# Six weights handed over transposed, bias rows on four column strips, and first loads split over two queues

## The chip, the cores and the metric

The kernel runs on one core of a Trainium2 chip. It is one program for the core's five engines: TensorE (PE in the profile), VectorE (DVE), ScalarE (ACT), GpSimd (POOL) and SyncE (SP, which here only issues DMAs). The metric is the device time of one execution in microseconds (us), as the median of several runs.

## What is computed

The input is `x`, 128 graphs of 64 nodes with 512 features (8192 tokens of 512, f32), an adjacency `adj` of 128x64x64 and a node mask. Four layers follow one another. Each adds to `x` what it makes of `h = relu(layernorm(x))`:

```
layer 0: q, k = split(h @ Wqk); v = h @ Wv
         w = mask * sum(q * (adj @ (k * mask))) / sqrt(512); x += softmax_nodes(w) * v
layer 1: q, k, v = h @ W.T + b   (three weights)
         w = adj * exp(q @ k.T);  x += (w / rowsum(w)) @ v
layer 2: q, k, v = h @ W.T + b;  8 heads; softmax(q k.T / 8 * 2 adj) @ v;  x += ctx @ Wo.T + bo
layer 3: e = leaky_relu(sj + si + ab); T = rownorm(adj * exp(e))
         x += relu(h Wk0 + T h Wk1 + T T h Wk2 + biases)
```

Layers 1 and 2 use their weights transposed (`W.T`). Layer 0 uses `Wqk` only through the product of its q half and its k half.

## The kernel before, in words

The 8192 tokens are cut into 16 groups of 512 (`NG = 16`). Layers 0 and 1 run in one loop over the groups, layer 1 one group behind layer 0; layer 2 and layer 3 have a loop each. Every engine has its own hand-written program (`pe_program`, `dve_program`, `act_program`, `pool_program`, `sp_program`); the order of the work is the order of the code, and semaphores join the engines. Matmul results go to eight PSUM banks that are handed out in rotation (`Banks.take`); a bank is written again only when the engine that read its last contents has said so.

A large f32 product is made in three passes: each operand is split into a part `hi` (rounded to float32r by ScalarE) and a part `lo` (the rest, by VectorE or GpSimd), and hi*hi, hi*lo and lo*hi are added up (L319 where a weight is the left operand, L329 where features are). So each weight needs, once, a `hi` and a `lo`. For a weight that is used as it lies in HBM (`v0`, the layer-3 weights) this is `split_in_place`: `hi` from `raw`, and then `lo` over `raw`, which has the same memory. For `v1`, `q2`, `k2`, `v2` and `o2`, TensorE first transposes the weight block by block into four banks (`split_T`, 16 transposes of 128x128, L296), and the split reads the banks (`split_W`).

Features: `stats_A` (DVE) and `scale` (POOL) give mean and scale, `norm` (ACT, L1002) makes `hn`, `transposes` (DVE, L668) turns it in blocks of 32x32 to `hs`, `gather` (SP, L1430) moves 16 blocks of 64 KB to `hGA` (layers 0, 2, 3) or `hGB` (layer 1), and from there `hi` (ACT, L988) and `lo` (POOL L1248, or DVE L631 in layer 2) are made. TensorE then starts the group.

The start, ahead of the first group: TensorE transposes the q half and the k half of `Wqk` (32 transposes, L296), ScalarE copies them to `qT` and `kTw`, and TensorE forms `m0` = q half times k half (`product`, L309, 16 f32 matmuls that are not split). Then come a sum of bias products (L405), two rows of bias times weight (L411: eight matmuls whose left operand is one column wide), the first half of the layer-1 product `a1` (L309), and group 0 (`l01_g0`). The other half of `a1`, the transposes of `v1` and the two small products `crow` (L472) and `ucol` (L476) stand behind group 0's `v0`. The bias columns and the mask columns are also made by TensorE transposes (L397, L398, and L437 for layer 2).

At the end of the first loop, round `g == NG`, stand the last layer-1 group and the preparations of layer 2: the transposes of `q2`, the product `l01_pv(14)` (attention times values; L380, L384), `g1` of group 15 (L319), the transposes of `k2`, `v1` of group 15 (L329) and its scores (L345). In the layer-2 loop follow the transposes of `v2`, `l01_pv(15)`, and at the end of group 0 those of `o2`.

```
for half in range(2):
    pe.wait_ge((d_qk0, d_qk1)[half], 16)
    for cc in range(4):
        transposed_blocks(("qkT", half, cc), wqk[:, :, half * 512:(half + 1) * 512], cc, ...)
```

## Time and profile before

| | |
|---|---|
| median of 3 runs | 2275.75 us (2275.45 to 2278.11) |
| profiled execution, its own time | 2281.91 us |
| its span, first to last instruction | 2280.1 us |
| TensorE busy | 2246.0 us (99%) |
| VectorE, ScalarE, GpSimd busy | 1314.0, 784.9, 717.8 us |
| mean granted TensorE clock | 0.995 |
| DMA over the span | mean 99 GB/s |

A busy share is time with at least one instruction of the engine running. Matmuls overlap and their ends are modelled, so the distance from one start to the next tells more than the length of one. In the chain of waits each row is a start, a length and who held up the end; rows are merged over neighbours. The granted clock is 1.00 at 2.4 GHz and 0.50 at 1.2 GHz; at the very start of the program it reads 1.00 whatever happens.

### The profile page before, as it was taken

What the parts mean: (1) busy time and instruction counts of PE and PEld (TensorE: products, weight loads), DVE (VectorE), ACT (ScalarE), POOL (GpSimd) and SP (SyncE); (2) the same over time, 40 slices, a digit from 0 to 9 for tenths busy, and PEclk for the clock granted to TensorE, in tenths of its full rate; (3) what the DMA queues carried; (4) which work ended last, traced back from release to release, by engine and by line L of the source; (5) the groups of instructions that cost most, each with busy time, mean ns of one, the idle gap of its engine ahead of it and who ended that gap; (6) DMA issues with size and microseconds to landing.
All of it is one profiled execution on the core that took longest, in us unless ns stands there. A gap on an engine that the chain in (4) does not pass through costs nothing.

```text
span 2280.1 us, 39533 instructions
## 1 busy us (share of the span) xinstructions
PE 2246.0 (99%) x15903; PEld 1779.9 (78%) x15903; DVE 1314.0 (58%) x2645; ACT 784.9 (34%) x1401; POOL 717.8 (31%) x926
## 2 busy tenths in 40 slices
PE   8999999999999999999999999999899999999998
PEld 5778888888888877888888888888677777777776
DVE  3565565565655665554656455665665757575752
ACT  3332332333322333233333333232343434343432
POOL 2343343334333423223332223332351313131320
PEclk9999999999999999999999999999899999999999
DMA  6223333333333343332333332333444343535341
GB/s 199 75 75 96 96 107 102 84 92 94 84 95 96 102 135 111 99 101 80 85 101 92 101 97 80 91 105 93 123 123 111 84 114 82 129 68 127 71 106 37
DMA packets 185048, 224.75 MB, mean 99 GB/s; under 512 B 68688, under 2 KB 85152, under 8 KB 184864
## 3 DMA queue, kind: packets, MB, share of 16 engines
q1 hardware_dynamic: 179104, 214.35, 35.1%
q10 hardware_dynamic: 5760, 7.87, 1.4%
q8 instruction: 125, 2.05, 0.4%
q14 instruction: 59, 0.48, 0.1%
HBM read 88.91 MB, written 50.37 MB: 61 GB/s over the span
## 4 chain that ended last, share of the span: by engine, by line
PE 90%; SPq 3%; DVE 3%; DMA 2%; ACT 1%; issue 1%; POOL 1%; DVEq 0%; ACTq 0%
PE bank L329 49%; PE bank L319 28%; PE bank L345 3%; PE bank L603 3%; SPq L1430 2%; PE bank L533 1%; PE bank L503 1%; PE bank L309 1%; PE bank L380 1%; DMA si<-stB 1%; PE bank L296 0%; DVE hs L668 0%; DMA arows<-stB 0%; DMA small<-in_L_gnn_ab 0%; ACT g1T L1037 0%
## 5 line engine op out<-in xcount | busy, mean ns | idle before, releaser
L329 PE MATMUL bank<-w_hi,h3T_hi 128*128 128x512 f32 x768 | 306.4, 399 | 1.8 <-ACT Z L988 1.8
L329 PE MATMUL bank<-w_lo,h3T_hi 128*128 128x512 f32 x768 | 300.3, 391 | 0.0
L329 PE MATMUL bank<-w_hi,h3T_lo 128*128 128x512 f32 x768 | 300.0, 391 | 0.0
L1235 POOL TENSOR_SCALAR stA<-stA 128x4 f32<-128x4 f32 x48 | 11.5, 239 | 682.8 <-DVE stA L645 682.7
L1002 ACT ACTIVATE hn<-x,stA 128x512 f32<-128x512 f32 x192 | 140.7, 804 | 233.9 <-POOL stA L1240 228.0
L643 DVE BATCH_NORM_STATS2 stA<-x 128x6 f32<-128x512 f32 x192 | 128.3, 668 | 149.2 <-DMA x<-mid 148.8
L329 PEld LDWEIGHTS bank<-w_hi,h3T_hi 128*128 128x128 f32 x768 | 144.7, 188 | 56.8 <-issue 25.2
L988 ACT ACTIVATE Z<-bank 64x512 f32<-64x512 f32 x256 | 151.7, 593 | 96.1 <-PE bank L329 78.8
L329 PEld LDWEIGHTS bank<-w_hi,h3T_lo 128*128 128x128 f32 x768 | 144.8, 188 | 30.6
L329 PEld LDWEIGHTS bank<-w_lo,h3T_hi 128*128 128x128 f32 x768 | 144.8, 189 | 29.0
L1248 POOL TENSOR_TENSOR h1T_lo<-hGB,h1T_hi 128x512 fp32r<-128x512 f32 x64 | 80.6, 1288 | 200.9 <-ACT h1T_hi L988 200.9
L668 DVE STREAM_TRANSPOSE hs<-hn 128x512 f32<-128x512 f32 x192 | 123.1, 687 | 17.8 <-ACT hn L1002 15.0
L969 DVE SCALAR_TENSOR_TENSOR junk<-hn,arowt 128x512 f32<-128x512 f32 x112 | 132.8, 1245 | 0.0
L631 DVE TENSOR_TENSOR cT_lo<-bank,cT_hi 128x256 fp32r<-128x256 f32 x128 | 44.8, 410 | 146.9 <-ACT cT_hi L988 146.9
L988 ACT ACTIVATE g0T<-bank 128x512 f32<-128x512 f32 x64 | 38.3, 598 | 239.1 <-PE bank L319 239.1
L825 DVE TENSOR_TENSOR x<-bank,x 128x512 f32<-128x512 f32 x64 | 43.3, 678 | 126.6 <-PE bank L329 126.3
L1116 ACT ACTIVATE QQ<-bank,stB 128x512 f32<-128x512 f32 x64 | 41.8, 687 | 196.8 <-issue 155.0
L1248 POOL TENSOR_TENSOR h3T_lo<-hGA,h3T_hi 128x512 fp32r<-128x512 f32 x64 | 106.2, 1688 | 0.1
L1132 ACT ACTIVATE zt<-zt 128x512 f32<-128x512 f32 x64 | 40.5, 632 | 188.8 <-POOL zt L1300 188.8
L329 PE MATMUL bank<-v_hi,h0T_hi 128*128 128x512 f32 x256 | 104.5, 408 | 0.0
L329 PE MATMUL bank<-o2w_hi,cT_hi 128*128 128x512 f32 x256 | 103.6, 405 | 0.6 <-DVE cT_lo L631 0.5
L1312 POOL TENSOR_TENSOR x<-x,blk 128x512 f32<-128x512 f32 x64 | 80.7, 1297 | 73.1 <-ACT hn L1002 73.1
(217 smaller groups left out, 5720.8 us busy)
## 6 DMA issues: line engine op xcount, KB each, us to landing
hGA<-hs SPq DMA_DIRECT2D x768, 64.0 KB, 2.0
mid<-x SPq DMA_DIRECT2D x32, 1024.0 KB, 4.5
x<-mid SPq DMA_DIRECT2D x32, 1024.0 KB, 6.2
x<-in_x SPq DMA_DIRECT2D x16, 1024.0 KB, 5.9
hGB<-hs SPq DMA_DIRECT2D x256, 64.0 KB, 2.0
out<-x SPq DMA_DIRECT2D x15, 1024.0 KB, 9.5
blk<-in_adj SPq DMA_DIRECT2D x128, 64.0 KB
PT<-hs SPq DMA_DIRECT2D x120, 64.0 KB, 2.1
```

What stands on the lines that cost most here:

```text
L319: ins = eng.matmul(b[:], W[l][:, k, os], h[r][:, k, :], start=(k == 0 and i == 0), stop=(k == 3 and i == 2))
L329: ins = eng.matmul(b[:], h[l][:, k, ts], W[r][:, k, :], start=(k == 0 and i == 0), stop=(last and k == 3 and i == 2))
L345: ins = eng.matmul(b[h, t * 64:(t + 1) * 64], left[:, k, ts], right[:, 2 * i:2 * i + 2, 4 * k + t, :], start=(k == 0), stop=(k == 3))
L603: ins = eng.matmul(b[HALF[c], :], left, Z[zi][h, 2 * r + c, :], start=False, stop=True)
L643: m = dve.step(eng.bn_stats(st[:, t, 0:6], xt[:, t, :]))
L668: eng.transpose(hs[:, :, :, t, :].rearrange("p b c r -> p c b r"), (hn1 if layer == 1 else hn)[t][:].rearrange("p (c b r) -> p c b r", c=4 ...
L969: eng.scalar_tensor_tensor(unused, hn[t][:], 0.0, arow[:, c, :], ALU.max, ALU.mult, accum_out=scol[g % 2][:, t, c:c + 1]).then_inc(v_dotA, 1)
L988: return eng.activation(dst, src, ACT.Copy)
L1002: eng.activation(h[t][:], xt[:, t, :], ACT.Relu, bias=st[:, t, 10:11], scale=st[:, t, 9:10]).then_inc(done, 1)
L1248: eng.tensor_tensor(by_token(h["lo"], q), hG[:, q], by_token(h["hi"], q).bitcast(F), ALU.subtract).then_inc(done, 1)
L1312: eng.tensor_tensor(xt[:, t, :], xt[:, t, :], bo2, ALU.add).then_inc(p_xb, 1)
L1430: eng.dma_start(hG[b * 32:b * 32 + 32, q].rearrange("p c r -> p (c r)"), hs[q * 32:q * 32 + 32, b].rearrange("p c t r -> p (c t r)")).then ...
```

## The change

The host now hands over six weights transposed in HBM (`L0_gnn_Wqk`, `L1_gnn_Wv_w`, and layer 2's `Wq`, `Wk`, `Wv`, `Wo`), four bias vectors as 128x4 columns, and a second copy of the node mask as 128x64 columns. All TensorE transposes of weights, biases and mask are gone; the five split weights use `split_in_place`, on DVE too. `Wqk` is loaded in four pieces straight into `qT` and `kTw`, and the product `m0` takes its four k steps outside and its four banks inside, so that the first half of the steps needs only the first two pieces. The two bias rows are made with a left operand 32 columns wide (`bsel`, zero but for its first column), each of four k steps on its own strip of 32 columns of the array and to its own 32 partitions; they are no longer added up by the bank but by the later products `crow` and `ucol`, which now contract over 128 partitions and not one. The first load of `x` is issued by ScalarE; of the 16 blocks of the first gather SP issues 8 and ScalarE 8, between its norms and its first copies out of the banks. `v1` is loaded ahead of that gather and not behind it. ScalarE and GpSimd split the features of group 0 before `v0`, and not after it.

```diff
-            for half in range(2):
-                pe.wait_ge((d_qk0, d_qk1)[half], 16)
-                for cc in range(4):
-                    transposed_blocks(("qkT", half, cc), wqk[...], cc, (a_qkT, 4 * half + cc + 1))
-            (bank "cols": two transposes of nm and brow1)
-            pe.wait_ge(a_qkT, 8)
-            product("m0", qT, kTw)
+            m0 = [bank.take(("wT", "m0", dc), (v_wlo, lo_dve["m0"] - 3 + dc)) for dc in range(4)]
+            for k in range(4):
+                pe.wait_ge((d_qk0, d_qk1)[k // 2], 32)
+                for dc, (b, full, _) in enumerate(m0):
+                    ins = eng.matmul(b[:], qT[:, k, dc * 128:(dc + 1) * 128], kTw[:, k, :], start=(k == 0), stop=(k == 3))
+                    if k == 3:
+                        ins.then_inc(full, 1)
...
-                    ins = eng.matmul(b[0:1, :], bcol[:, c0 + k:c0 + k + 1], w[:, k, :], start=(k == 0), stop=(k == 3))
+                    ins = eng.matmul(b[32 * k:32 * k + 32, :], bsel[:, c0 + k, :], w[:, k, :], start=True, stop=True,
+                                     tile_position=(0, 32 * k))
...
-                    pe.wait_ge(d_q2, 16)
-                    split_T("q2", Wq2["raw"])
-                        pe.wait_ge(d_k2, 16)
-                        split_T("k2", Wk2["raw"])
-                    pe.wait_ge(d_v1, 16)
-                    split_T("v1", wv1)
-                    eng.matmul(b[:], ones1[0:1, :], crow1[:], start=True, stop=True).then_inc(full, 1)
+                    eng.matmul(b[:], ones1[:], crow1[:], start=True, stop=True).then_inc(full, 1)
-                    pe.wait_ge(d_v2, 16)
-                    split_T("v2", Wv2["raw"])
-                    pe.wait_ge(d_o2, 16)
-                    split_T("o2", Wo2["raw"])
...
+            def split_in_place(W, name):                        # DVE
+                for k in range(4):
+                    dve.wait_ge(a_whi, hi_of[name] - 3 + k)
+                    lo_split(W["lo"][:, k, :], W["raw"][:, k, :], W["hi"][:, k, :]).then_inc(v_wlo, 1)
...
+        def blocks(eng, hG, qs):
+            for q in qs:
+                for b in range(4):
+                    eng.dma_start(hG[b * 32:b * 32 + 32, q].rearrange("p c r -> p (c r)"),
+                                  hs[q * 32:q * 32 + 32, b].rearrange("p c t r -> p (c t r)")).then_inc(d_h[q], 16)
...
-            for half, dst in enumerate((qT, kTw)):               # ACT
-                for cc in range(4):
-                    copy(dst[:, cc, :], bank.of(("qkT", half, cc))[:]).then_inc(a_qkT, 1)
+            eng.dma_start(xs[0][:], x_v[0]).then_inc(d_x[0], 16)
             norm_A(0, 0)
+            act.wait_ge(v_tr, 4)
+            blocks(eng, hGA, (2, 3))
             split_W(Wm0, "m0")
+            features2_hi(0, 0, hT[0])
             split_in_place(Wv0, d_v0)
-            features2_hi(0, 0, hT[0])
...
+            for h, loaded in enumerate((d_qk0, d_qk1)):          # SP
+                eng.dma_start(qT[:, 2 * h:2 * h + 2, :], qk_rows[:, 2 * h:2 * h + 2, :]).then_inc(loaded, 16)
+                eng.dma_start(kTw[:, 2 * h:2 * h + 2, :], qk_rows[:, 4 + 2 * h:6 + 2 * h, :]).then_inc(loaded, 16)
+            eng.dma_start(bcol[:, 0:4], L1_gnn_Wq_b).then_inc(d_b1, 16)
```

The places where the order of instructions changes, as the programs have it. The first is TensorE at the start of the program, before (names: `bank<-kTw,qTw` is `m0`, `bank<-wq,wk` is `a1`, and `h0T`, `m` are the first group's features and the weight `m0`):

```order
1 L296 MATMUL bank<-ident,wqk 128x128 x32
2 L397 MATMUL bank<-ident,nm 128x64
3 L398 MATMUL bank<-ident,brow 128x8
4 L309 MATMUL bank<-kTw,qTw 128x512 x16
5 L405 MATMUL bank<-bprod,ones 128x4
6 L411 MATMUL bank<-wk,bcol 1x512 x4
7 L411 MATMUL bank<-wq,bcol 1x512 x4
8 L309 MATMUL bank<-wq,wk 128x512 x8
9 L319 MATMUL bank<-h0T_hi,m_hi 128x512
```

And TensorE at the same place in the changed program:

```order
1 L380 MATMUL bank<-kTw,qTw 128x512 x16
2 L386 MATMUL bank<-bprod,ones 128x4
3 L391 MATMUL bank<-wk,bsel 32x512 x4
4 L391 MATMUL bank<-wq,bsel 32x512 x4
5 L296 MATMUL bank<-wq,wk 128x512 x8
6 L306 MATMUL bank<-h0T_hi,m_hi 128x512
```

The 34 transposes ahead of `m0` are gone, the row products have 32 rows and not one, and the rest stands as it stood.

ScalarE at the start of the changed program, with its share of the first loads and blocks:

```order
1 L1017 DMA x<-in_x 128x4x512
2 L972 ACT_TABLE_LOAD
3 L972 ACTIVATE hn<-x,stA 128x512 [waits scaleA]
4 L972 ACTIVATE hn<-x,stA 128x512 x3
5 L951 DMA hGA<-hs 32x512 [waits tr]
6 L951 DMA hGA<-hs 32x512 x7
7 L958 ACTIVATE m_hi<-bank 128x512 [waits bank_full0]
```

Before, eight copies to `qTw` and `kTw` stood in place of the first DMA, and no DMA stood between the norms and `m_hi`.

TensorE at the end of the first loop, before: behind `v1` of group 14 come the transposes of `q2`, then `l01_pv(14)`, and then `g1` of group 15.

```order
3163 L329 MATMUL bank<-v_hi,h1T_lo 128x512
3164 L437 MATMUL bank<-ident,amt 128x8
3165 L296 MATMUL bank<-ident,q2w_raw 128x128 x16
3166 L380 MATMUL bank<-vf,ext 64x257 x2
3167 L384 MATMUL bank<-vf,ext 64x256 x2
```

The same place in the changed program:

```order
3159 L316 MATMUL bank<-v_hi,h1T_lo 128x512
3160 L367 MATMUL bank<-vf,ext 64x257 x2
3161 L371 MATMUL bank<-vf,ext 64x256 x2
```

`l01_pv(14)` now stands directly behind `v1` of group 14; nothing else in this round moves on TensorE but the 16 transposes of `k2` that leave their place between `g1` and `v1` of group 15.

## Rows read from the trace of the kernel before

**Rows 1.** The page, busy time, share and instructions of TensorE and the others.
```profile
PE 2246.0 (99%) x15903; PEld 1779.9 (78%) x15903; DVE 1314.0 (58%) x2645; ACT 784.9 (34%) x1401; POOL 717.8 (31%) x926
```
**Rows 2.** Chain of waits, 0 to 135 us: start, length (us), what.
```profile
6.07 6.13 PE bank L296 x28
...
13.36 14.00 PE bank L309 x32
...
27.47 6.96 PE bank L411 x16
34.43 7.06 PE bank L309 x16
41.49 10.93 PE bank L319 x48
...
72.94 1.75 PE bank L296 x16
```
**Rows 3.** The tile wqk, DMA issues to landing.
```profile
DMA to landing us min/median/max: 5.2/5.9/7.5
```
**Rows 4.** Windows at the start: busy per engine, clock, DMA share, GB/s.
```profile
4.00:8.00 4.00, 1.93 (x9) 1.96 (x10) 0.00 (x0) 0.60 (x1) 0.00 (x0) 1.00 1.05 396
```
**Rows 5.** Timeline, 0 to 40 us: start, length, engine, line, what [idle before].
```profile
13.42 0.69 DVE L643 BATCH_NORM_STATS2 stA<-x 128x6 f32<-128x512 f32 x1
...
19.72 2.83 DVE L668 STREAM_TRANSPOSE hs<-hn 128x512 f32<-128x512 f32 x4 [3.01 <-ACT hn L1002]
...
22.58 10.82 SPq L1430 DMA_DIRECT2D hGA<-hs  x16
...
33.49 4.95 POOL L1248 TENSOR_TENSOR h0T_lo<-hGA,h0T_hi 128x512 fp32r<-128x512 f32 x4
```
**Rows 6.** Chain of waits, 1560 to 1760 us, at the start of layer 3.
```profile
1705.74 5.49 PE bank L329 x12
1711.22 2.17 PE bank L603 x16
...
1735.41 1.88 PE bank L603 x16
```
**Rows 7.** Windows of TensorE: busy (x), granted clock, DMA share, GB/s.
```profile
1642.00:1645.00 3.00, 0.93 (x4) 0.75 0.00 0
1706.00:1709.00 3.00, 3.00 (x8) 0.50 0.00 0
```
**Rows 8.** Chain of waits, 800 to 960 us, end of layer 1.
```profile
823.84 2.72 PE bank L329 x12
...
839.13 2.04 DMA hGB<-hs
...
841.90 1.27 POOL h1T_lo L1248
...
854.39 1.75 PE bank L296 x16
...
869.28 1.75 PE bank L296 x16
```
**Rows 9.** Timeline of VectorE, 820 to 935 us.
```profile
836.99 0.69 DVE L804 TENSOR_TENSOR vf<-bank,bv 128x512 f32<-128x512 f32 x1 [2.03 <-PE bank L329]
...
869.32 0.69 DVE L804 TENSOR_TENSOR vf<-bank,bv 128x512 f32<-128x512 f32 x1 [2.03 <-PE bank L329]
```
**Rows 10.** Timeline of TensorE, in 836 to 912 us, and at 1644 us.
```profile
840.51 0.43 PE L380 MATMUL bank<-vf,ext 64*64 64x257 f32 x2 [0.48 <-DVE q2w_lo L631]
...
843.22 0.50 PE L319 MATMUL bank<-h1T_hi,a_hi 128*128 128x512 f32 x1 [1.54 <-POOL h1T_lo L1248]
...
909.03 1.91 PE L296 MATMUL bank<-ident,o2w_raw 128*128 128x128 f32 x16
911.62 0.50 PE L319 MATMUL bank<-h2T_hi,q2w_hi 128*128 128x512 f32 x1 [0.68 <-DVE h2T_lo L631]
...
1644.07 1.09 PE L513 MATMUL bank<-ident,zt 128*128 128x128 f32 x4 [3.79 <-POOL zt L1304]
```

More of the change, by code:

```diff
@@ L289, in pe_program @@
             pe = Queue(eng, s_pe)
-            def transposed_blocks(key, src, cc, freed):
-                b, full, before = bank.take(key, freed)
-                if before:
-                    pe.wait_ge(*before)
-                for r in range(4):
-                    ins = eng.transpose(b[:, r * 128:(r + 1) * 128], src[:, r, cc * 128:(cc + 1) * 128], ident[:])
-                ins.then_inc(full, 1)
-            def split_T(name, src, ccs=range(4)):
-                for cc in ccs:
-                    transposed_blocks(("wT", name, cc), src, cc, (v_wlo, lo_dve[name] - 3 + cc))
             def product(name, l, r, dcs=range(4)):
@@ L432, in pe_program @@
                     l01_g0(g, (0, 1))
-                else:
-                    b, full, before = bank.take(("bqk",), (v_bqk, 1))
-                    pe.wait_ge(*before)
-                    pe.wait_ge(d_b2, 32)
-                    eng.transpose(b[:, 0:8], brow2, ident[0:8, 0:8]).then_inc(full, 1)
-                    pe.wait_ge(d_q2, 16)
-                    split_T("q2", Wq2["raw"])
                 if on_pv:
@@ L475, in pe_program @@
                     for d in range(4):
[L476 removed]
+                        ins = eng.matmul(b[:, d:d + 1], urow[:, d * 128:(d + 1) * 128], ones1[:, 0:1], start=True, stop=True)
                     ins.then_inc(full, 1)
@@ L633, in split_W @@
             def split_W(W, name, ccs=range(4)):
-                if name in ("v1", "q2", "k2", "v2", "o2"):
-                    dve.wait_ge(*bank.done(("wT", name, 3)))
                 for cc in ccs:
@@ L745, in dve_program @@
                 dve.wait_ge(*bank.done(("rows1", j)))
-                eng.tensor_copy(row[:], bank.of(("rows1", j))[0:1, :]).then_inc(v_rows1, 1)
+                eng.tensor_copy(row[:], bank.of(("rows1", j))[:]).then_inc(v_rows1, 1)
             split_W(Wa1, "a1", (0, 1))
@@ L751, in dve_program @@
                 if g == NG:
-                    dve.wait_ge(*bank.done(("bqk",)))
-                    eng.tensor_copy(bqk, bank.of(("bqk",))[:, 0:8]).then_inc(v_bqk, 1)
-                    split_W(Wq2, "q2")
+                    split_in_place(Wq2, "q2")
                 if on_pv:
@@ L1074, in act_program @@
                         l01_zexp(1)
-                        act.wait_ge(*bank.done(("wT", "v1", 3)))
                         features2_hi(1, 0, hT[1])
@@ L1285, in pool_program @@
                 else:
-                    pool.wait_ge(*bank.done(("wT", "v1", 3)))
+                    pool.wait_ge(*bank.done(("wT", "a1", 3)))
                     pool.wait_ge(v_wlo, lo_dve["v1"])
@@ L1406, in load0, with gather @@
                     load_adj(g)
-            def gather(layer, g):
+            def gather(layer, g, qs=range(4)):
                 if g >= NG:
@@ L1427, in gather @@
                 sp.wait_ge(v_tr, 4 * kT(layer, g) + 4)
-                for q in range(4):
-                    for b in range(4):
-                        eng.dma_start(hG[b * 32:b * 32 + 32, q].rearrange("p c r -> p (c r)"),
-                                      hs[q * 32:q * 32 + 32, b].rearrange("p c t r -> p (c t r)")).then_inc(d_h[q], 16)
+                blocks(eng, hG, qs)
             def gather_pT(g):
@@ L1639 @@
     for name in _INS:
-        a = _np.ascontiguousarray(inputs[name])
+        a = inputs["nodemask" if name == "nodemask_cols" else name]
+        if name in _TRANSPOSED:
+            a = _np.transpose(a)
+        if name in _COLUMNS:
+            a = _np.reshape(a, (-1, 128)).T
+        a = _np.ascontiguousarray(a)
         arrays[f"in_{name}"] = a
```

101 lines of the change are left out of this document (42 added, 59 removed).

## The prediction

> **What bounds the kernel now.** I read the page first: TensorE is busy for 2246.0 of 2280.1 us [rows 1], so an instruction taken from it is worth its length, unless TensorE waits right behind it for something else. The question is therefore where its 34 us of idle time lie. I took TensorE's waits, then the chain of waits at the start and at the end of layer 1, and there the timelines. Some 6 us of idle time lie ahead of the first matmul; in the first loop there is next to none, so what is gained at the start stays gained: every later load, gather and copy is released by something that TensorE has done. Two spots have idle time right behind removed work. One is 843.22, where g1 of group 15 waits 1.54 us for GpSimd; the other is 911.62, where layer 2's second group waits 0.68 us for VectorE [rows 10].
>
> **The start.** Before, the first weight half, issued at 0.7, lands 5.2 us later, at 5.9, and the second one, issued half a us behind it, takes 7.5: 8.7 [rows 3]. TensorE transposes from 6.07, `m0` runs from 13.36 for 14.00, the bias rows from 27.47 for 6.96, the first half of `a1` from 34.43 for 7.06, and group 0 begins at 41.49 [rows 2].
>
> First data. The first two pieces of q and k are together 1 MB, as much as one half was. But `x`, 1 MB too, is now under way beside them, issued by ScalarE at about the same time. The engines move 396 GB/s at 4 to 8 us with a busy share of 1.05 [rows 4]: they are full with one queue. So a second queue takes from the first. If both get the same share, pieces and `x` land when 2 MB had landed before, at 8.7; if `x` gets nothing at first, at 5.9. I take 8.7. The Trainium skill says the same (DMA: Bandwidth & Descriptors, Issuing engines are not separate DMA queues): transfers issued from several engines run on the same 16 DMA engines and interleave, and only the issue time is saved. By that rule this part of the change brings nothing to the first matmul and costs it 2.8 us; somebody who counts on two queues giving twice the rate would have it start at 5.9.
>
> Clock. The transposes at the start ran at half the later pace: 28 in 6.13 us, or 219 ns each, against 16 in 1.75 us, or 109 ns, at 72.94 [rows 2]. The array was still at 1.2 GHz although the granted clock shows no step there, and 28 x 109 ns = 3.1 us was the useful part. Nobody paid for this but the transposes; now the first matmuls of `m0` stand there. The only other slow stretch with large matmuls is at the start of layer 3: at a granted clock of 0.50 [rows 7] 12 matmuls took 5.49 us and the next product 2.17 [rows 6], against 2.72 [rows 8] and 1.88 [rows 6]. That is 3.06 us lost. Both ends: 0 (clock up at once) to 3.1. Both rows give 3.1, and I take 3.0: `m0` takes 14.0 + 3.0 = 17.0. The second pieces land while the first half is being worked on, 8.7 us or more, so they cost nothing.
>
> Bias rows. Eight f32 matmuls of 512 columns, 16 records, 6.96 us. The trace has no strips of 32 columns. Nearest is L603: 64x64 tiles, 512 columns, 16 records in 1.88 us [rows 6], so four tiles at work at once. Ends: 1.9 us (four strips as four tiles) and 7.0 (one after the other). I take 1.9. The Trainium skill measured less for strips that share a direction (TensorE: Matmul & The Clock Gate, Measured speedup vs the span model): 3.07 times for four row strips; that would make it 2.3 us, and by it the sum would be 0.4 us smaller. L603, the row of this kernel, decides.
>
> So TensorE: 8.7 + 17.0 + 0.1 (bias sum) + 1.9 + 7.06 = 34.8, against 41.49: 6.7 us gained, if the features are there.
>
> Features. Before, DVE begins on `x` at 13.42, held by the mask columns, and its transposes end at 22.55 (19.72 + 2.83), 9.1 us later; the 16 blocks take 10.82 us to issue; GpSimd ends at 38.44 [rows 5]. After: `x` at 8.7, transposes done at 17.8, 8 issues on each of two engines 5.4 us, so 23.2, plus 2 us to land: 25.2. SP's 8 blocks lie behind all weights: 7.5 MB at 396 GB/s from about 2.5 us are through at 22.4, so they fit too. ScalarE is busy with its issues until 23.2 and then has the four `m0` banks, the last of which is full at 25.7: 26.3. GpSimd starts 0.7 us after ScalarE's first feature copy and takes 4.95: 26.3 + 0.7 + 5.0 = 32.0. That is 2.8 us before 34.8. GpSimd's v0 split now stands behind; it ends at about 37, and v0 is needed at 34.8 + 10.9 = 45.7. No cost.
>
> **`v1`, `crow`, `ucol`.** The 16 transposes, 1.75 us on the chain [rows 2], go. Contraction over 128 partitions streams the same columns: 0. The chain goes from these transposes through crow and ucol into group 1 without a wait for features, and the features of group 1 hang on group 0's scores and last v0, which move along; some of their cover goes, and how much is left must show. Gain 1.75.
>
> **End of layer 1.** `q2`: in front of g1 of group 15 the chain does not run over TensorE but over 16 block issues, the landing at 841.17, and GpSimd, which ends at 843.17 [rows 8]. Nothing there is removed. Gain 0; the idle time grows instead. `k2`: 1.75 us between busy matmuls [rows 8]; what follows (v1 of group 15) waits for nothing new, and its scores, which need g1's last copy by ScalarE, come a whole v1 piece of 2.72 us behind. Gain 1.75. `v2`: before, pv(15) starts at 871.03 (869.28 + 1.75) [rows 8]. It needs the last `vf`, which VectorE ends at 870.01 (869.32 + 0.69) [rows 9]. So it can come 1.0 us earlier, and 0.75 becomes a wait. Gain 1.0. `o2`: TensorE waits for h2T_lo, made at a distance from KK's copies that nothing shortens. Gain 0; the wait grows from 0.68 to 0.68 + 1.9 = 2.6 us [rows 10].
>
> The ACT and DVE halves of the splits are as many and as long; they read SBUF and not a bank, at their old places. The bias and mask transposes fall into the parts counted.
>
> **Sum.** 6.7 + 1.75 + 1.75 + 1.0 = 11.2 us. On the profiled execution that is 2281.91 - 11.2 = 2270.7; the runs' median is 6.2 us below the profiled one, so the time is 2275.75 - 11.2 = 2264.5 us. With both favourable ends (first data at 5.9 and full clock at once) TensorE would be ready at 29.0, the features then hold it (ready some 3 us after `m0`'s eviction at best, 31.4, since they hang on `x` at 8.7): 10.1 + 4.5 = 14.6, or 2261.2. With strips one after the other it is 11.2 - 5.1 = 6.1, or 2269.6.
>
> **Rivals.**
> - *The clock falls in the gap at 843.* After the change pv(14) starts when the last vf is done (836.99 + 0.69 = 837.7) [rows 9]. Its second half took 1.17 us (840.51 to 841.68, where the wait of 1.54 begins) [rows 10], so the whole is 2.3 and ends at 840.0. Then TensorE is idle for 3.2 us. At 1640.3 it was idle for 3.79 us [rows 10] and the clock had fallen by 1643.5 (0.75 over 1642 to 1645) [rows 7], 3.2 us in. It is a close call, and pv is thin work besides. Price 3.06 us as above: 2267.6. Against it: the gap is the shorter one, and the 1.54 us at 843 left no mark before. The gap of 2.6 us at 911 is of the same kind and less likely. Chance 0.22.
> - *The strips do not run at once.* Then the rows take 7.0 us: 2269.6. Against it stands L603. Chance 0.08.
> - *First data at 5.9, or a quick clock.* The sum grows by up to 3.4 us: 2261.2. For it: ScalarE also has its table to load at its start, which may put `x` behind. Chance 0.2.
> - *The two queues disturb one another.* If the DMA engines moved half as much with two queues to serve (198 for 396 GB/s), the 7.5 MB of weights and `x` and the 1 MB of blocks would take from 2.5 to 47.5 us. SP's eight blocks are the last of it, so ScalarE and GpSimd finish near 52, and group 0 begins 10.5 us later than before; less 4.5 us of the later gains that is 6.0 us slower: 2281.8. It turns the change into a loss from the point where group 0's features come later than 46.0 (41.49 + 4.5). Against it: two queues share, and nothing in the trace loses rate. Chance 0.02.
>
> **How the numbers follow.** The forecast as summed has 0.48, the rivals 0.22, 0.08, 0.2 and 0.02. The range from 2260.5 to 2269.5 takes in the quick start, the fallen clock and about the strips; it leaves out the disturbed queues, and misjudged covers. A measurement of this kernel can tell 0.2%, 4.6 us, from no change; only the strips and a fallen clock together (3.0 us gained), or a cost not seen here, come under this. Faster 0.93, within 0.2% 0.05, slower 0.02.
>
> **What would show it.** In the new profile: first matmul near 8.7, `m0` with its first records twice as far apart, the row products in about 1.9 us, and group 0 near 34.8 with no wait for GpSimd ahead of it; group 1 8.4 us earlier; at 835 (the old 843.22) no earlier start relative to the scores of group 14, with about 3 us idle ahead of it; `k2` 1.75 and `v2` 1.0 less. I am wrong if group 0 waits for features, if the bias rows take over 2.5 us, if the granted clock reads below 1 near 835 us, or if the loop over groups has new waits.

## The result, and the profile after

The changed kernel takes 2282.0 us (median of 11 runs, 2276.7 to 2284.8), the kernel before 2276.0 on the same chip: ratio 1.0021, 95% interval 1.0013 to 1.0029. On a second occasion, with both kernels unchanged, it was 2284.4 against 2277.4: 1.0026 (1.0013 to 1.0038). The forecast was 2264.5. The changed kernel is 6 to 7 us slower where 11.2 us of gain were expected, so 17 to 18 us are missing.

The page of the changed kernel, the row of busy times and the chain that ended last (share of the span by engine, then by line):

```profile
PE 2230.5 (98%) x15788; PEld 1767.0 (78%) x15788; DVE 1317.8 (58%) x2643; ACT 780.9 (34%) x1393; POOL 722.9 (32%) x927
...
PE 78%; DVE 8%; SPq 5%; DMA 5%; POOL 1%; issue 1%; ACT 1%; DVEq 0%; ACTq 0%; POOLq 0%
```

TensorE is busy for 15.5 us less than in [rows 1], and yet the end is not earlier. The second row says why. The same row of the kernel before, profiled again, and of the changed one, profiled again:

```profile
PE 89%; SPq 3%; DVE 3%; DMA 2%; ACT 1%; issue 1%; POOL 1%; DVEq 0%; ACTq 0%
```
```profile
PE 78%; DVE 8%; SPq 6%; DMA 5%; POOL 2%; issue 1%; ACT 1%; DVEq 0%; POOLq 0%; ACTq 0%
```

A tenth of the span has moved from TensorE's account to VectorE, SyncE's queue and transfers. The chain of the steady part of the last layer alone, 1720 to 2270 us, kernel before (again), then the changed kernel:

```profile
by line: PE bank L329 88.3%; PE bank L603 10.1%; PE bank L589 1.1%; DVE yt L952 0.4%; issue 0.2%; DVE x L954 0.0%
```
```profile
by line: PE bank L316 49.5%; SPq L951 12.2%; DVE junk L933 10.5%; DMA x<-mid 8.6%; PE bank L567 5.7%; DVE stA L610 3.2%; DVE hs L635 3.0%; issue 1.7%; POOL stA L1206 1.3%; ACT hn L972 1.3%; DVE stA L612 0.9%; PE bank L553 0.7%; POOL stA L12
```

Before, TensorE alone sets the pace of that layer. After, a ring of other engines takes part in it: SyncE issues 16 blocks (L951), then the load of `x`, then VectorE's statistics (L610), scaling, normalising, VectorE's transposes (L635), VectorE's sums (L933), and back to SyncE. TensorE isn't in that ring. TensorE's waits in the stretch, of the changed kernel (total us, times, longest; `alt` is what the row sums of L553 read):

```profile
PE bank L553 <- POOL alt L1310: 5.6, 3, 2.3
```

and its busy time there (us, then each engine's busy time and count, clock, DMA share, GB/s), kernel before (again), then changed:

```profile
1720.00:2260.00 540.00, 540.00 (x2578) 409.11 (x2577) 329.90 (x573) 218.71 (x384) 137.95 (x136) 1.00 0.37 94
```
```profile
1720.00:2260.00 540.00, 534.30 (x2540) 403.00 (x2539) 330.24 (x573) 216.78 (x380) 138.33 (x136) 1.00 0.36 94
```

38 matmuls fewer fit into the same 540 us: at 0.227 us from one to the next that is 8.6 us. The three waits are 5.6 us of it; part of the rest is the clock, which the trace has at 0.50 at 1963.5 to 1966.5 us, behind the third wait (in `a_again` behind two of the three).

To see where time is lost I paired the matmuls of two profiles one by one (leaving out the transposes and anything added) and took the difference of their start times. The table gives how many us TensorE is ahead of the kernel before, profiled again, at the same matmul, with that kernel's time in the head. Names of the experiments are explained below. Each row is one execution, and the kernel before itself has two: `before` is the profile that the forecast was made from, at the end 5.2 us behind the one that the table is measured against.

```
profile       839    913   1233   1621   1648   1711   2267 (end)
after         7.5    5.9    5.5    6.2    5.6    6.0   -2.4
a_again       9.2    8.9    9.2    9.9    7.9    2.9   -8.5
before       -0.6   -0.5   -0.5   -1.8   -2.3   -5.0   -5.2
a_early      10.6    9.7    9.1    9.8    7.1    4.9    4.9
a_warm        7.3    8.6    8.9    9.6    7.9    6.4    6.4
a_best       10.1   10.9   11.1   11.9    9.7    2.9    2.9
a_pad         3.1    2.9    3.2    3.9    2.5    3.4    0.2
a_fill3       6.6    5.6    5.8    6.6    4.4   -7.6   -9.2
b_fill3       0.1   -1.2   -1.2   -1.3   -1.3   -8.8   -8.8
a_tr4         5.7    5.7    5.7    3.6    3.8   -2.1   -2.1
b_v4          0.8    0.6    0.9   -0.8   -0.6   -2.1   -3.9
b_p64        -0.2   -0.2   -0.2   -1.1   -1.5   -3.4   -4.1
a_p115        7.4    7.8    7.4    4.4    4.9   -5.5  -13.9
a_p115_blk    7.7    7.5    7.8    2.6    6.4    1.8   -8.5
a_p115_si     4.2    4.0    4.3    2.4    3.1   -1.7   -9.4
```

So the gain is real up to 1620 us, 6 to 10 us, and the two profiles of the changed kernel lose it in two places: on the way out of layer 2 (1621 to 1711: 0.2 and 7.0 us) and in the last layer (1711 to the end: 8.4 and 11.4 us). The first place isn't peculiar to the changed kernel: `before` loses 3.2 us there.

**The start.** The rows that answer to [rows 2, 5], timeline of TensorE in the changed kernel:

```profile
9.15 16.51 PE L380 MATMUL bank<-kTw,qTw 128*128 128x512 f32 x32 [9.15 <-DMA kTw<-in_L_gnn_Wqk]
25.50 0.28 PE L386 MATMUL bank<-bprod,ones 128*128 128x4 f32 x2
25.71 1.06 PE L391 MATMUL bank<-wk,bsel 128*32 128x512 f32 x8
...
36.43 0.50 PE L306 MATMUL bank<-h0T_hi,m_hi 128*128 128x512 f32 x1 [1.73 <-POOL h0T_lo L1216]
```

and the chain behind that last wait:

```profile
0.72 7.97 DMA x<-in_x
8.71 0.70 DVE stA L610
...
15.02 2.84 DVE hs L635 x4
...
19.79 10.90 DMA hGA<-hs
30.71 0.64 ACT h0T_hi L958
31.41 4.98 POOL h0T_lo L1216 x4
```

`x` lands at 8.7, `m0` takes 16.5, the bias rows of 16 records begin at 25.71 and the next product at 27.57: three steps as forecast. The last one isn't: a block issued at 19.8 is at hand only at 30.7. The transfer engines are full in that time (share and GB/s stand last):

```profile
20.00:24.00 4.00, 4.00 (x11) 1.82 (x10) 0.03 (x1) 0.61 (x2) 0.00 (x0) 1.00 1.06 358
24.00:28.00 4.00, 4.00 (x23) 1.48 (x22) 3.64 (x7) 1.77 (x3) 0.00 (x0) 1.00 1.08 247
```

### The profile page after: what moved, and what is told of

It is laid out like the page before. It is cut to its first block, busy times and chain, and to the rows that moved or that the text cites. A ratio compares the mean times of both kernels' runs of the same rounds, so it can differ in the third digit from the quotient of the medians.

```text
span 2277.4 us, 39277 instructions
## 1 busy us (share of the span) xinstructions
PE 2230.5 (98%) x15788; PEld 1767.0 (78%) x15788; DVE 1317.8 (58%) x2643; ACT 780.9 (34%) x1393; POOL 722.9 (32%) x927
## 4 chain that ended last, share of the span: by engine, by line
PE 78%; DVE 8%; SPq 5%; DMA 5%; POOL 1%; issue 1%; ACT 1%; DVEq 0%; ACTq 0%; POOLq 0%
PE bank L316 40%; PE bank L306 29%; SPq L951 5%; DVE junk L933 3%; PE bank L332 3%; DMA x<-mid 2%; PE bank L502 1%; PE bank L567 1%; PE bank L472 1%; PE bank L367 1%; DVE hs L635 1%; DVE stA L610 1%; DMA hGA<-hs 1%; DMA si<-stB 0%; DVE yt L933 0%
## 5 line engine op out<-in xcount | busy, mean ns | idle before, releaser
L610 DVE BATCH_NORM_STATS2 stA<-x 128x6 f32<-128x512 f32 x192 | 128.3, 668 | 160.4 <-DMA x<-mid 151.2
L316 PEld LDWEIGHTS bank<-w_hi,h3T_hi 128*128 128x128 f32 x768 | 144.8, 189 | 56.6 <-issue 25.2
L635 DVE STREAM_TRANSPOSE hs<-hn 128x512 f32<-128x512 f32 x192 | 124.1, 689 | 19.5 <-ACT hn L972 19.3
L933 DVE SCALAR_TENSOR_TENSOR junk<-hn,arowt 128x512 f32<-128x512 f32 x112 | 133.5, 1252 | 0.0
L1084 ACT ACTIVATE QQ<-bank,bqk 128x512 f32<-128x512 f32 x64 | 42.1, 688 | 205.2 <-issue 155.0
L306 PE MATMUL bank<-h1T_hi,a_hi 128*128 128x512 f32 x256 | 100.5, 392 | 5.3 <-POOL h1T_lo L1216 5.3
```

The costliest lines, as they stand in the source:

```text
L306: ins = eng.matmul(b[:], W[l][:, k, os], h[r][:, k, :], start=(k == 0 and i == 0), stop=(k == 3 and i == 2))
L316: ins = eng.matmul(b[:], h[l][:, k, ts], W[r][:, k, :], start=(k == 0 and i == 0), stop=(last and k == 3 and i == 2))
L610: m = dve.step(eng.bn_stats(st[:, t, 0:6], xt[:, t, :]))
L635: eng.transpose(hs[:, :, :, t, :].rearrange("p b c r -> p c b r"), (hn1 if layer == 1 else hn)[t][:].rearrange("p (c b r) -> p c b r", c=4 ...
L933: eng.scalar_tensor_tensor(unused, hn[t][:], 0.0, arow[:, c, :], ALU.max, ALU.mult, accum_out=scol[g % 2][:, t, c:c + 1]).then_inc(v_dotA, 1)
```

## The experiments

Eighteen runs followed, in five batches, two of them of the unchanged kernels; each ratio compares with runs of the kernel before on the same chip. Chips differ (that kernel's median lay between 2276.0 and 2279.6 us), so medians of different batches are compared through it.

### Both kernels again, and the ring

> The kernel before once more, unchanged. All theories: ratio 1.000, median near 2276 us. Its second profile says how far the one read for the prediction (2281.91 us) was an outlier: the first profile lies 6 us above the median of the timed runs. If the missing 6 us lie in the passage from layer 2 to layer 3 (clock falls at 1644 and 1706), layer 3 begins about 6 us earlier in this profile and the changed kernel's lead there is 5 and not 11 us.

> The changed kernel once more, unchanged. Median near 2282 us, spread 8 us against 3 for the kernel before. Ring theory (layer 3 is held by a ring of load, statistics, transposes, sums, 16 block issues on SP, next load, of 36.6 us plus stalls against 37.3 for TensorE): its first matmul of layer 3 is earlier than before's, and by the end the lead is gone; TensorE has idle time in layer 3. Clock theory (the new gaps make the clock fall, and that is the whole loss): TensorE has no idle time in layer 3 and the lead lost lies at 837 and 906 us.

The kernel before: 2277.24, ratio 0.9999 (0.999 to 1.0008). The changed one: 2284.38, 1.0026.

`a_early` and `b_early` move one load of the ring in either kernel:

```
             for g in range(NG):
                 ...
                 sums_in3(g + 1)
+                load3(g + 3)
                 sums_out3(g + 2)
                 gather(3, g + 2)
-                load3(g + 3)
```

> The changed kernel with layer 3's load of x for group g+3 issued ahead of the gather of group g+2 and not behind it, so that 10 us of block issues and 6.5 us of landing drop out of the ring. Ring theory: TensorE is continuous in layer 3, and the time falls by 8 to 14 us, to 2268 to 2274. Clock theory: nothing changes by over 2 us, about 2281.

> The kernel before with the same earlier load in layer 3. Ring theory: it had cover, TensorE had no idle time there, so 0 to 2 us less than 2276. If it gains as much as the changed kernel does, then the ring bound before as well and the lead of the changed kernel is not lost there but before it.

`a_early`: 2274.45, ratio 0.9988 (0.9979 to 0.9997), 10 us under the changed kernel and just above the range expected. `b_early`: 2278.06, 1.0002 (0.9993 to 1.0011), nothing. TensorE's last layer is without a wait again, and the chain of that stretch is TensorE's:

```profile
by line: PE bank L316 87.4%; PE bank L567 10.1%; PE bank L553 1.1%; DVE yt L916 0.5%; issue 0.3%; DVE x L918 0.1%
```

The lead on entering the layer, 4.9 us, is the lead at the end. The ring is a cause in the changed kernel and not in the one before: there TensorE came just late enough not to see it.

### TensorE's slack in the last layer

```
             for g in range(NG):
                 i = g % 2
+                if g == 1:
+                    for _ in range(31):
+                        eng.matmul(b[:], w2_hi[:, 0, 0:128], w2_hi[:, 1, :], start=True, stop=True)
```

> The changed kernel with 31 matmuls of 128x512 (7.0 us at 0.227 us each) that nothing reads, on TensorE at the start of group 1 of the last layer. Ring theory (in the last layer of the changed kernel TensorE is ahead of SyncE's ring of blocks, x load, sums, and what TensorE is early by is waited away before row sums): TensorE waited 5.6 us for alt after that place in one profile and 6.7 in the other, beside 3.4 us of low clock that the waits brought, so 4 to 7 of the 7 us are hidden, and the kernel comes to 2282 to 2286, at most 3 over the changed kernel, with waits for alt under 2 us. Rival (the layer is 8 to 11 us longer because TensorE's own work is slower there, by low clock or matmuls): 7 over it, 2289 to 2291, and the waits stay.

> The same 31 matmuls at the same place of the kernel before. There TensorE's chain has no wait over 1 us from 1709 to 2267 us, so both theories say +7: 2281 to 2284. If it is under 3, the last layer of the kernel before isn't bound by TensorE, and the ring theory has its premise wrong.

`b_fill3`: 2284.01, 1.0029 (1.0018 to 1.0039), 6.8 us more, the full 7. `a_fill3`: 2277.59, 1.0006 (0.9997 to 1.0015), under the 2282 to 2286 expected: 7 us of added work cost nothing, and the ratio is below the changed kernel's. That it is lower can't come from the ring; the edit also lengthens TensorE's program, which is looked at below. TensorE's busy time in the same 540 us, `a_fill3` (the added matmuls stand ahead of this stretch, at 1709 to 1716 us):

```profile
1720.00:2260.00 540.00, 539.05 (x2564) 408.93 (x2563) 329.70 (x573) 217.15 (x381) 137.84 (x136) 1.00 0.37 95
```

The same edit costs its whole length in one kernel and nothing in the other: in the last layer of the changed kernel TensorE isn't the bound. The table says it without medians: this profile, the slowest of the kernel's twelve runs (2285.92), enters the layer 10.5 us later than `a_again` and ends 0.7 us later.

### What the ring loses

Without a stop the ring takes 36.2 to 36.6 us a group (VectorE's first statistics, 1723.83 to 1760.34 to 1796.96 in the changed kernel), TensorE 37.3, so the ring has less than 1.2 us to spare. But one of its 16 issues now and then takes 3 instead of 0.59 us. Chain of the changed kernel:

```profile
1819.95 2.59 SPq L951
1822.54 0.04 issue
1822.59 0.59 SPq L951
...
1824.49 2.95 SPq L951
```

That interval was 40.9 us. Over twelve intervals the ring's mean is 37.7 and 37.6 us in the two profiles of the changed kernel, 37.6 and 37.2 in those of the kernel before. Where the trace shows such an issue, it mostly shows within 0.5 us a transfer of the queues that it lists as `instruction` (q8 and q14 on the page), loads of the engines' programs. What SyncE's issues between 1720 and 2250 us took beyond 0.6 us each adds up to 24.5 us in the changed kernel (27.8 again), and to 19.2 in the kernel before (18.8 again). The sum counts issues off the ring too: in `a_early`, where TensorE waits for nothing, it is 29.9.

`a_pad` adds 12 small loads in the first loop, so that SyncE's later DMAs lie further on in its program:

```
                     load_blocks(0, g)
+                if g == 3:
+                    for i in range(12):
+                        eng.dma_start(pad1[:, 4 * i:4 * i + 4], L2_gnn_bq).then_inc(d_pad, 16)
```

> The changed kernel with 12 small loads more (4 columns each into unused memory) on SyncE in group 3 of the first loop, where it is idle: all that SyncE issues later lies 12 DMAs further on in its code. Code theory (the stalls of 2.6 to 3.4 us in issues of the last layer, the same four in three profiles, counted from the last DMA back at 337, 262, 217 and 26, are fetches of code at fixed places): the stalls stand 12 DMAs earlier, at about 349, 274, 229 and 38 from the end; 349 and 274 then lie outside or at the edge of the 16 blocks. The sum of stalls over 0.6 us in 1720 to 2250 (24.5 and 27.8 us in the changed kernel, 19 in the one before) moves by some us either way and the time by up to 4: 2278 to 2286. Rival (stalls come from where other traffic happens to be): the same positions or random ones, time 2282 to 2284.

2276.49, 0.9995 (0.9987 to 1.0004): some 7 us better against the kernel before than the changed kernel is, and under the range expected, from 12 loads that nobody reads. SyncE wasn't idle for them: they stood ahead of a load of `x`, and TensorE lost 3 us of lead at 240 to 270 us. Counted from the last DMA back, the stops at 262 and 26 are gone, those at 337 and 217 are where they were (3.6 and 3.4 us), and none stands at 349, 274, 229 or 38. So the theory that these stops are loads at fixed places of SyncE's own code isn't borne out. The time did move, but this edit shifts when everything later happens as well as SyncE's code, so it doesn't show which of the two did it.

### The clock in the two gaps

`a_warm` is `a_early` with 14 unread matmuls in the wait before the last group of the first loop and 8 before layer 2's second group.

> The changed kernel with the last layer's load of x ahead of the blocks (2274.5 in the earlier run), and with matmuls that nothing reads in two waits of TensorE: 14 of 0.227 us in the wait of 3.8 us ahead of the last group of the first loop (833 us), 8 in the wait of 2.4 us ahead of group 1 of layer 2 (901 us). Clock theory: no fall at 833 and 901, each of which cost 1.2 to 2 us (9 records 0.20 us further apart at the first): group 1 of layer 2 begins 2.5 to 3.5 us earlier than 900.7, and as the last layer is bound by TensorE in this kernel most of it stays: 2271 to 2273. Rival (what is won by then is lost on the way into the last layer, as 5 of 10 us were): 2274 to 2275.

2272.81, 0.9984 (0.9975 to 0.9992). The changed kernel around the gap (busy times, clock), then `a_warm`:

```profile
830.00:836.00 6.00, 1.99 (x33) 1.31 (x32) 4.40 (x4) 4.38 (x8) 4.75 (x4) 1.00 0.38 96
836.00:840.00 4.00, 2.72 (x6) 2.15 (x7) 3.86 (x8) 0.00 (x0) 1.23 (x1) 0.61 0.74 262
```
```profile
832.00:836.00 4.00, 4.00 (x33) 3.02 (x26) 3.54 (x3) 2.62 (x5) 4.00 (x4) 1.00 0.48 105
836.00:840.00 4.00, 3.54 (x16) 2.58 (x15) 3.86 (x8) 0.01 (x1) 0.86 (x1) 1.00 0.78 256
```

And around layer 2's second group:

```profile
902.00:905.00 3.00, 0.69 (x3) 0.60 (x4) 3.00 (x6) 1.99 (x4) 0.00 (x0) 1.00 0.00 0
905.00:908.00 3.00, 3.00 (x9) 2.37 (x8) 3.00 (x6) 0.00 (x0) 0.00 (x0) 0.52 0.04 11
```
```profile
904.00:908.00 4.00, 4.00 (x19) 3.29 (x18) 4.00 (x8) 0.00 (x0) 0.00 (x0) 1.00 0.42 99
```

The clock is at its lower level behind both gaps in the changed kernel and at its higher one in `a_warm`. Some 8 matmuls stand 0.43 instead of 0.23 us apart there, 1.6 us a fall. The leads show it: from 839 to 1233 us `a_early` goes from 10.6 to 9.1 and `a_warm` from 7.3 to 8.9, 3.1 us apart for two falls. The medians don't: they differ by 1.6 us, but the intervals of the two kernels overlap, and `a_warm`'s lead was 3.3 us smaller to begin with.

### Either part alone

`b_v4` is the kernel before with the four weights of layer 2 handed over transposed (`split_T` and the waits for the bank taken out, `split_in_place` put in). `a_tr4` is the changed kernel with just these four transposed on TensorE as before.

> The kernel before with the transposes part alone, for the four weights of layer 2 (q2, k2, v2, o2); v1 and the start as before. Ring theory: the gap at 840 us stays without its 16 transposes, so by the start of layer 2's group 1 the lead over the kernel before is 1 to 3 us (k2 1.5, v2 0.9, a clock fall of 1 to 2 taken off), and the last layer, where before's TensorE is only 0 to 2 us behind the ring, takes most of it: 2275 to 2278, no change. Sum theory (what is gained stays): 2273 to 2274.5.

> The changed kernel with those four weights handed over as before and transposed on TensorE again, so the start part and v1 alone. At group 1 of layer 2 its lead over the kernel before is some 7 us (904 to 905), no clock fall at 837. If the loss comes with the lead alone, it comes back here too, since the lead on entering the last layer is 3 to 5 us: 2280 to 2285. If the loss comes from where the fetches of code fall among the blocks (other engines' programs are of the old length here), the time is 2273 to 2279. Sum theory: 2270.

`b_v4`: 2282.06, 1.0021 (1.0012 to 1.003). `a_tr4`: 2278.69, 1.0006 (0.9997 to 1.0015). `b_v4` is a miss for both theories; `a_tr4` lies in the range given for the one on where code is loaded, and under that of the ring. Taking out 64 transposes alone makes the kernel before 5 us slower. In the table 1.8 us of that go in the last layer, at a wait for `alt`:

```profile
PE bank L579 <- POOL alt L1336: 1.5, 1, 1.5
```

The other 3.0 us go between 1233 and 1711 us. On the way out of layer 2 TensorE has an unexplained 2.02 us in the chain ("issue" is time in which the engine waited for nothing that the profile shows):

```profile
1649.00 3.69 PE bank L528 x128
1652.69 1.80 PE bank L329 x5
1654.49 2.02 issue
1656.50 19.82 PE bank L329 x79
```

### SyncE's first blocks ahead of later weights

`a_best` is `a_warm` with the loads of Wv1, bv1 and layer 2's biases behind SyncE's first eight blocks; `a_best2` adds unread matmuls on the way out of layer 2 (3 ahead of each of the last four transposed pieces, 14 ahead of the last context products).

> The kernel with the early load of x and the matmuls in two waits (2272.8), and SyncE's first eight blocks ahead of the loads of Wv1, bv1 and layer 2's biases. In the changed kernel the blocks landed at 30.7 us, behind the weights, and group 0 began at 36.43, 34.95 and 34.27 in three profiles, with waits for the features; with the blocks first they land by 28, and group 0 begins at 34.1 to 34.4. Queue theory: 0.5 to 2 us of the start, 2271 to 2272.5. Rival (the blocks wait for ScalarE's own eight in the transfer engines): 2272.8.

> a_best with matmuls that nothing reads at the way out of layer 2 too: 3 ahead of each of the last four transposed pieces and 14 ahead of the last group's context (where TensorE waits 4 us and the clock is low for 7 to 17 us). The runs of these kernels fall in two clusters some 7 us apart, with mean clocks of 0.996 and 0.993 (2270 and 2277): if the upper cluster is a longer low stretch at that place, as 17.1 us in one profile of the changed kernel against 6.8 in another, it goes: all runs 2268 to 2272. If the clusters come from elsewhere, they stay, and the median is that of a_best or 1 us over it, since the fillers stand in a chain that DVE sets.

`a_best`: 2271.33, 0.9974 (0.9965 to 0.9983); group 0 begins at 34.14 without a wait (35.25 with a wait of 1.8 us in `a_warm`). `a_best2`: 2271.79, 0.9975: no more. `a_best` is the fastest version, 5.6 us under the kernel before and about 11 under the changed one.

### The length of TensorE's program

If the place at which TensorE's code is loaded decides, the old length should bring the old time. The padding is one-column matmuls ahead of TensorE's first wait:

```
             pe.wait_ge(c_pool, 1)
+            for _ in range(64):        # 64, 93 or 115
+                eng.matmul(bank.tiles[0][0:1, 0:4], ident[:, 0:1], ident[:, 0:4], start=True, stop=True)
```

> The kernel before with four weights of layer 2 handed over transposed (2282.1, 5 over the kernel before), and 64 one-column matmuls that nothing reads ahead of TensorE's first wait, where it is idle until 6 us: TensorE's program has its old length again. Code theory (b_v4 lost its 5 us on the way out of layer 2, where a load of 16 KB of TensorE's code at 1655.2 to 1656.4 coincides with two stops of TensorE in its output products, 3.6 us more than in the kernel before; 64 instructions pairs fewer moved that load from where it did no harm): 2274 to 2277.5. Rival (the missing transposes themselves, by timing or the clock at 844, cost it): 2281 to 2283.

> The kernel before, unchanged but for the same 64 one-column matmuls ahead of its first wait: the work is the same, only TensorE's code lies half a 16 KB load further on (a load comes every 27 us, in which TensorE has some 119 matmuls at 0.227 us). Code theory: half a load further or half a load back is the same place, so 2280 to 2283 as b_v4 was, with the stop of 2 to 5 us at 1650 to 1657. Rival: 2276 to 2278.

> The changed kernel with 115 one-column matmuls ahead of TensorE's first wait (idle until 9.15 us), which give TensorE's program its length of before. 115 is nearly one whole load of code, so by the code theory TensorE's stops lie 13 matmuls from where the changed kernel has them, in the passage out of layer 2 as in the kernel before (no stop, a late load beside it): the profiles of the changed kernel had a stop of 0 and of 4.7 us there; with it gone in all runs the time is 2277 to 2281. If only the ring of the last layer is at fault, 2282 to 2284. If the start is delayed by the added matmuls (nearest row: 64x64 matmuls 0.03 us apart, 115 of them 3.5 us, the idle time is 7.5), 1 to 2 more.

> a_best (2271.3) with 93 of these matmuls at the start, which with its 22 fillers give TensorE's program its old length. Code theory: a_best's profile had low clock 3.4 and 6.8 us more in the passage than a_warm's, and its runs spread from 2266.3 to 2274.5; without a stop of TensorE there the median is 2268 to 2270. Rival: 2271 to 2272, no change.

The kernel before took 2279.64 beside these four. `b_v4_p64`: 2287.66, 1.0037 (1.0024 to 1.0049). `b_p64`: 2279.78, 1.0000. `a_p115`: 2291.49, 1.0059 (1.0046 to 1.0073). `a_best_p93`: 2281.66, 1.0008. The theory falls: half a load further changes nothing in the kernel before, and the old length makes the others slower still. `a_p115` is 12 us over the kernel before, which is 5 to 6 more than the changed kernel; 1 of these is at the start (`m0` begins at 10.1). Its lead falls most between 1621 and 1711 us, by 9.9. The chains there show one stop in the last context products of layer 2 (softmax times values, 128 products of 64x64). `a_again`, then `a_p115`:

```profile
1640.55 3.06 PE bank L502 x80
1643.60 4.72 issue
1648.33 0.98 PE bank L502 x24
```
```profile
1643.55 3.22 PE bank L504 x106
1646.77 5.46 issue
...
1652.56 0.92 PE bank L504 x21
```

`a_tr4`, `a_fill3` and `a_best_p93` have it too (4.0 to 4.8 us), `a_best2` has 1.7 us of it, `b_v4_p64`, `a_best` and `b_v4` have a shorter one (3.1, 2.8 and 2.0 us) in the output products just behind; `after`, `a_warm`, `a_pad` and the kernel before, padded or not, have none, and `a_early` has 0.5 us. The runs of one kernel may differ in it as well, but no run shows this: `a_early`'s times lie at 2271.8 to 2274.5 and 2277.2 to 2278.7, and its one profile was among the lower ones.

### What stops TensorE there

In the nine profiles so far with a stop of over 1 us it ends 8.6 to 9.9 us after SyncE has issued the first sums of the last layer, 2 KB in 512 pieces of 4 bytes (`si` from `stB`), with four adjacency loads of 64 KB right behind. Two kernels, made from `a_p115`, take these out of that place:

```
 a_p115_blk:  if g == NG - 1:
+                 load_blocks(3, 0)
                  sums_out3(0)
-                 load_blocks(3, 0)

 a_p115_si, beside that:
-                 sums_out3(0)
                  ...
                  if g == NG - 1:
                      for a in range(2):
                          sp.wait_ge(*bank.done(("ctx", g, 1, a)))
+                     sums_out3(0)
                      eng.dma_start(W3[0]["raw"][:], rows(L3_gnn_Wk[0])).then_inc(d_w0, 16)
```

> The changed kernel with the 115 one-column matmuls at the start (2291.5), and on SyncE the last layer's first four adjacency loads (64 KB each) ahead of the small transfer of sums (si from stB) instead of right behind it. Six profiles have a stop of TensorE of 4 to 5.5 us in the context products of layer 2's last group; it ends 8.8 to 9.9 us after the issue of that small transfer, and in four of them a load of 16 KB of TensorE's code took 5.5 to 8.9 us there, 1.2 in the mean. Sums theory (the code waits behind the small transfer's 512 pieces of 4 bytes): the stop stays, from 4 us to 9 or 10 us after that issue, and the time is 2289 to 2292. Blocks theory (it waits behind the adjacency loads, issued 0.4 us later): the stop is gone, 2284 to 2287.

> The same with the small transfer of sums as well moved, behind SyncE's wait for TensorE's last context product, so that it is not on its way while these products need code. Sums theory: no stop of TensorE in the context products, so TensorE starts the last output products 5 us earlier; the sums arrive some 5 to 8 us later, at about 1666, and the first row sums may wait for them up to 4 us: 2284 to 2289. Blocks theory: no difference to a_p115_blk. Rival to both (the stop is neither's, but the length of the program): the stop stays at the same products in both, 2291.

`a_p115_blk`: 2286.76, 1.0044 (1.003 to 1.0057), `a_p115_si`: 2286.44, 1.0043 (1.003 to 1.0056), with the kernel before at 2276.75 on this chip; `a_p115` had 1.0059 (1.0046 to 1.0073). SyncE's queue and TensorE's chain, `a_p115_blk`:

```profile
1640.82 0.38 SPq L1433 DMA_DIRECT2D si<-stB  x1
```
```profile
1642.08 3.22 PE bank L504 x106
1645.30 3.22 issue
```

and `a_p115_si`, where the 128 products run through:

```profile
1653.50 0.44 SPq L1433 DMA_DIRECT2D si<-stB  x1
```
```profile
1645.32 3.69 PE bank L504 x128
```

With the sums alone in flight the stop stays, 3.2 us instead of 5.5, and ends 7.7 us after their issue; with neither it is gone. It is one profile each, and several profiles of other kernels were without a stop, so this supports the sums as the cause and the adjacency loads as an addition; it doesn't prove it. And the sums can't be behind every such stop: most profiles have another, of 0.5 to 3.4 us, among the score products (queries times keys) at 1610 to 1625 us, 25 us or more ahead of them. `a_p115`:

```profile
1615.98 2.61 PE L474 MATMUL bank<-KK,QQ 64*64 64x64 f32 x99 [3.43 <-issue]
```

In total the two kernels stand 10 us over the kernel before, 2 us less than `a_p115` by the medians, and the intervals overlap, so a gain in time isn't shown. In `a_p115_si` row sums wait for the later sums. Their last layers lose 10.3 and 7.7 us to the ring, as in the changed kernel.

## Why the forecast was wrong, step by step

- **First data, `m0`, bias rows: right.** 8.7 forecast and 9.15 found; 17.0 and 16.5, with the first records twice as far apart; 1.9 and 1.86. TensorE alone would have been ready at 34.7, against 34.8.
- **Features at 32.0: wrong by 4.4 us.** They came at 36.4, and TensorE waited 1.7 us for them (0.5 and 0 in the profiles of `a_again` and `a_early`). The step took the weights as through at 22.4 us, at 396 GB/s; the last one, issued at 12.1, landed at 26.2, and SyncE's blocks were at hand at 30.7, not 25.2. SyncE was slow to issue (3.29 us for the mask loads alone), but that didn't leave the transfer engines idle: their busy share is 1.03 or more in every 4 us from 4 to 32 us, at 247 to 389 GB/s. So it was the rate, taken from the best 4 us of the kernel before, that failed. With the blocks ahead of the later weights (`a_best`) there was no wait.
- **`v1` 1.75: right.** The lead grows by 2.0 to 2.1 us across its place in the three profiles `after`, `a_again` and `a_early`; at group 1 of the first loop it was 6.7 to 8.7 us, against 8.4.
- **`q2` and `o2`, gain 0: the rival on the clock came true.** The wait came to 4.4 instead of 3.2 us, and the clock fell behind it in these three profiles, in two of them behind the gap at 905 too. Priced at 3.06 us, it was 1.6 a time. I had given it 0.22; it was likely, and small.
- **`k2` and `v2`: right.** The lead grows by 1.7 and by 1.0 us across their places, against 1.75 and 1.0. The lead in layer 2 was 5.9 to 9.7 us, where 11.2 less the late features (0 to 1.7) and two falls of the clock (3.2) gives 6 to 8, or 9.6 with one.
- **The sum on the end: wrong.** The step that failed is the sentence on what bounds the kernel: "what is gained at the start stays gained: every later load, gather and copy is released by something that TensorE has done". That held in the first two loops, up to 1620 us. In the last layer the load of `x`, the blocks, the sums and the next blocks release one another without TensorE, in 36.2 to 36.6 us without a stop against TensorE's 37.3; with its stops the ring's mean is above, 37.7 us. That TensorE had next to no idle time ([rows 1], 99%) said only that TensorE came later than the ring, not by how much. 8.4 and 11.4 of the 17 to 18 us went there (shown by `a_early`, `b_early`, `a_fill3` and `b_fill3`).
- **The loss beyond zero** isn't explained by a ring alone, which would end no later than before. The ring of the changed kernel had more long issues (24.5 and 27.8 us beyond 0.6 an issue, against 19), though its mean of 37.7 and 37.6 us is clearly above only one of the two profiles of the kernel before (37.2; the other has 37.6). And there is the stop on the way out of layer 2 in some of the profiles. Edits that add no work of weight moved the time by 0 to 8 us, in either direction: 115 matmuls 5 to 6 slower, 93 of them 8 slower, 64 of them 3 slower or nothing, 12 loads 7 faster. They change program lengths and timing together, and I found no rule for where the stops fall. So the cause of the part that makes the kernel slower than before stays open, and so does why `b_v4` is slower by 5 us.
- **The rival on the other side** gave 2281.8 us, near the result, but for two queues at the start that halve the rate to 198 GB/s. No profile shows that, and TensorE's lead behind the start was 6.7 to 8.7 us in the first three profiles. It was right by accident.

## What to carry to other kernels

Before a gain on the busiest engine is carried to the end, look in every stage for the loops that don't pass through that engine, and compare their period with its own. A zero wait hides a margin of 1% as well as one of 50%. Where work is taken out in front of a wait, price the clock behind the longer gap, or leave cheap work in it. When a change of a few tenths of a per cent also changes the length of the programs, run a version padded elsewhere before believing the sign.

## What the hardware showed that I had not expected

- The profile lists loads of the engines' programs (`instruction`, q8 and q14) among the transfers of the DMA engines. Those of q8 are 16 KB; they are taken here for TensorE's, since there are 124 in the changed kernel, 125 in the kernel before and 126 in `b_p64` and `a_p115`. They took 1.2 us in the mean, but 5.5 to 8.9 us in five profiles (`a_tr4`, `b_v4_p64`, `a_best_p93`, `b_again`, `b_p64`) while the 512 pieces of 4 bytes were on their way. TensorE goes through 128 products of 64x64 in 3.7 us there, and stops for up to 5.5 us. In `b_again` and `b_p64` the same late load stopped nothing in these products, and in `a_again`, `a_fill3` and `a_p115` the trace has a stop and no such load in it, so how the two hang together stays open. (The text on record ahead of `a_p115_blk` has four such loads beside a stop, of up to 8.9 us; that of 8.9 us, in `b_p64`, had none beside it.)
- Single DMA issues of SyncE take up to 5.7 us instead of 0.59 in the last layer. Over the twenty profiles, 141 of 148 that took more than 1.2 us lie within 0.5 us of such a load (q8 or q14).
- 115 matmuls of one column at the start, which delayed the first product by 1 us, made a kernel 5 to 6 us slower, and 12 small loads in the first loop, which cost TensorE 3 us there, made it 7 us faster.
- Expected, but in no row before: four 32-column strips of 512 columns run at once. 8 matmul records take 1.06 us.
